# Half-array turns of the attention probabilities, beside the scores, and a new order of slots

## What is computed

```python
x = x + tanh(g_xattn[1]) * _L1_xattn_ref(_layernorm(x), ctx, ctx, Wq, Wk, Wv, Wo, bo)
#   16 heads of 64: attn = softmax(q @ k.T * 64**-0.5); out = concat(attn @ v) @ Wo + bo
x = x + tanh(g_ffn[1]) * _L1_ffn_ref(_layernorm(x), centroids, biases, Ws_up, Ws_down, W_up, W_down)
#   shared = silu(x @ Ws_up) @ Ws_down; top 8 of 64 experts by x @ centroids.T; weighted sum
```

## Time and profile before

| | us |
|---|---|
| median of 3 runs | 2946.25 (2937.28 to 2954.1) |
| profiled execution, span from first to last instruction | 2561.4 |
| outside the span, by the median | 384.85 |
| PE busy | 2366.4 (92% of the span) |
| DVE busy | 1692.1 (66%) |
| ACT busy | 1525.4 (60%) |
| POOL busy | 729.2 (28%) |

### The profile page before, as it was taken

The page is one execution under the profiler, slowest core; times in us unless marked ns, Lnnn a source line. Parts: engine busy times, 40 slices in busy tenths (PEclk is TensorE's granted clock), DMA queues, the critical chain, the costliest instruction groups (busy, mean ns, idle before and its releaser), DMA issues. The chain is left out here.

```text
span 2561.4 us, 63498 instructions
## 1 busy us (share of the span) xinstructions
PE 2366.4 (92%) x20058; PEld 1795.7 (70%) x20059; DVE 1692.1 (66%) x5327; ACT 1525.4 (60%) x4611; POOL 729.2 (28%) x863
## 2 busy tenths in 40 slices
PE   7999999999998999999999999999999869999950
PEld 5777777777776566666666666666666658888840
DVE  4776776777674567767667767766776645555559
ACT  3777777777773656656666666665665425545530
POOL 2000000000000023322322332332332347777740
PEclk8999999999999999999999999999999989999975
DMA  5111111111113211111111111111110366666659
GB/s 155 44 36 48 46 36 48 45 42 42 45 35 95 72 30 47 42 35 41 42 40 37 42 44 32 47 42 30 47 42 28 110 211 187 186 186 188 188 186 380
DMA packets 145288, 210.06 MB, mean 82 GB/s; under 512 B 23976, under 2 KB 108506, under 8 KB 145026
## 3 DMA queue, kind: packets, MB, share of 16 engines
q1 hardware_dynamic: 114322, 139.92, 18.7%
q0 software_dynamic: 26544, 60.21, 7.0%
q10 hardware_dynamic: 4160, 6.55, 0.7%
HBM read 118.21 MB, written 96.75 MB: 84 GB/s over the span
## 5 line engine op out<-in xcount | busy, mean ns | idle before, releaser
L1454 ACT ACTIVATE wup<-bank,nmax 112x375 f32<-112x375 f32 x512 | 297.3, 585 | 127.2 <-DVE nmax L1558 126.0
L766 ACT ACTIVATE prob<-bank,nmax 112x375 f32<-112x375 f32 x512 | 293.6, 586 | 55.7 <-DVE nmax L850 51.6
L850 DVE TENSOR_REDUCE nmax<-bank 112x1 f32<-112x375 f32 x512 | 255.4, 541 | 90.2 <-PE bank L588 90.2
L2045 POOL DMA_INDIRECT expert_results<-res,dest x288 | 280.2, 973 | 118.5 <-ACT res L2163 67.0
L1558 DVE TENSOR_REDUCE nmax<-bank 112x1 f32<-112x375 f32 x512 | 255.4, 541 | 36.0 <-PE bank L1250 36.0
L1895 POOL DMA_INDIRECT expert_rows<-rows,ids x248 | 237.2, 957 | 78.6 <-issue 69.0
L2163 ACT ACTIVATE res<-bank,xr 128x256 f32<-128x256 f32 x288 | 136.4, 474 | 190.7 <-PE bank L2077 189.6
L1868 POOL TENSOR_TENSOR stats<-stats,neg_half 112x1 f32<-112x1 f32 x64 | 35.7, 557 | 654.6 <-DVE stats L1589 652.2
L1313 PE MATMUL bank<-wup,wk 128*128 128x375 f32 x512 | 219.8, 512 | 2.1 <-DMA wup<-context_turned 0.9
L1019 POOL TENSOR_TENSOR stats<-stats,neg_half 112x1 f32<-112x1 f32 x64 | 35.1, 549 | 633.7 <-DVE stats L880 629.7
L1460 ACT COPY pT<-bank 128x336 f32<-128x336 f32 x512 | 201.1, 449 | 19.7 <-PE bank L1257 19.1
(11 more groups left out here) (255 smaller groups left out, 5001.6 us busy)
## 6 DMA issues: line engine op xcount, KB each, us to landing
xr<-expert_rows SPq DMA_DIRECT2D x288, 129.0 KB
wup<-expert_results SPq DMA_DIRECT2D x14, 1024.0 KB, 18.8
wdn<-expert_results SPq DMA_DIRECT2D x14, 1024.0 KB, 20.2
wdn<-in_L_ffn_W_down_dram SPq DMA_DIRECT2D x8, 1024.0 KB, 12.2
expert_rows<-nowhere SPq DMA_DIRECT2D x56, 129.0 KB, 3.1
x_and_h_in<-stage SPq DMA_DIRECT2D x32, 224.0 KB, 2.6
xt<-x_and_h_in SPq DMA_DIRECT2D x32, 224.0 KB, 2.8
context_turned<-ctxT SPq DMA_DIRECT2D x32, 187.5 KB, 2.3
```

The costliest lines, as they stand in the source:

```text
L766: nc.scalar.activation(prob[:, n % RING, :NK], s_bank[r][:NQ, :NK], ACT.Exp, bias=nmax[:, r:r + 1], accum_out=rsum[:, par, h:h + 1]).then_ ...
L850: nc.vector.tensor_reduce(nmax[:, r:r + 1], s_bank[r][:NQ, :NK], AX, ALU.max, negate=True).then_inc(maxed, 1)
L1454: nc.scalar.activation(prob[:, n % RING, :NK], s_bank[r][:NQ, :NK], ACT.Exp, bias=nmax[:, r:r + 1], accum_out=rsum[:, par, n:n + 1]).then_ ...
L2045: nc.gpsimd.indirect_dma_start(results_d, bass.IndirectOffsetOnAxis(ap=dest[:, n % DEST:n % DEST + 1], axis=0), res[:, n % RES, :], None, ...
```

## The change

Turning goes by two heads at once, and in two halves: rows 0 to 63 and 64 to 111 of the probabilities are turned separately, each in its half of the array's rows, into a bank of its own (bank 4 takes six blocks of 64 columns, bank 5 six of 48). ACT copies each bank in one instruction for both heads. A quarter begins with the turns of two heads, then come the next scores, then the turns of the other two, and all slots follow. `ORDER_C` is laid anew (no job changes its lane; no slot n of a quarter is used). ACT takes the router's exponential out of the router's slot to the end of the third quarter; DVE takes the four maxima of a quarter in one piece ahead of the slots, and `shared_silu` goes from slot 9 to 11.

```diff
 ORDER_C = [
-    (1, "post", "va3", "dve"), (1, "own", "v10", "act"), (1, "own", "v11", "dve"),
+    (1, "post", "va3", "dve"), (1, "own", "v10", "act"), (1, "post", "wo", "dve"), (2, "own", "v12", "act"),
...
-                def turn(i, n):
-                    wait_kept(pe, i, n - 1)
-                    pe.wait_ge(exped, H * i + n + 1)
-                    for c in range(KC):
-                        mm = pe.transpose(pt_bank[n % 2][:, c * NQ:(c + 1) * NQ],
-                                          prob[:, n % RING, c * P:(c + 1) * P], ident[:NQ, :NQ])
+                def turn_pair(i, n):
+
+                    wait_kept(pe, i, n)
+                    pe.wait_ge(exped, H * i + n + 2)
+                    for a in range(2):
+                        for c in range(KC):
+                            at = a * KC + c
+                            for half, rows_of in enumerate((slice(0, HALF_Q), slice(HALF_Q, NQ))):
+                                width = rows_of.stop - rows_of.start
+                                mm = pe.transpose(pt_bank[half][:, at * width:(at + 1) * width],
+                                                  prob[rows_of, (n + a) % RING, c * P:(c + 1) * P], ident[rows_of, rows_of])
                     mm.then_inc(turned, 1)
...
                         uses.run(hooks, i, n, par, first, last)
+                        turn_pair(i, n)
                         next_scores(i, par, g, last)
+                        turn_pair(i, n + 2)
                         uses.run(hooks, i, n + 1, par, first, last)
-                        turn(i, n)
-                        turn(i, n + 1)
                         uses.run(hooks, i, n + 2, par, first, last)
-                        turn(i, n + 2)
-                        turn(i, n + 3)
                         uses.run(hooks, i, n + 3, par, first, last)
...
+                    to = pT[:, n % PT_RING:n % PT_RING + 2, :].rearrange("p a (c q) -> p (a c) q", c=KC)
+                    for half, (start, stop) in enumerate(((0, HALF_Q), (HALF_Q, NQ))):
+                        width = stop - start
+                        nc.scalar.copy(to[:, :, start:stop],
+                                       pt_bank[half][:, :2 * KC * width].rearrange("p (a q) -> p a q", q=width)).then_inc(kept, 1)
...
+                        uses.run(hooks, i, n, par, first, last)
+                        keep_pair(i, n)
+                        keep_pair(i, n + 2)
+                        next_exponentials(i, par, n, last)
+                        uses.run(hooks, i, n + 1, par, first, last)
+                        next_exponentials(i, par, n + 1, last)
                         tanhs(i, n, last)
...
+                        next_exponentials(i, par, n + 2, last)
                         uses.run(hooks, i, n + 2, par, first, last)
-                        next_exponentials(i, par, n + 2, last)
                         next_exponentials(i, par, n + 3, last)
-                        tanhs(i, n + 3, last)
+                        if n == 8 and not first:
+                            sigmoid_exp(i - 1)
                         uses.run(hooks, i, n + 3, par, first, last)
...
-                parts_y = [(2, moments_y), (4, norm_y), (9, choose), (11, sigmoids), (12, weigh), (9, shared_silu),
+                parts_y = [(2, moments_y), (4, norm_y), (9, choose), (11, sigmoids), (12, weigh), (11, shared_silu),
...
-                        next_maximum(i, par, n, last)
-                        next_maximum(i, par, n + 1, last)
-                        next_maximum(i, par, n + 2, last)
+                        for m in range(4):
+                            next_maximum(i, par, n + m, last)
```

More of the change, by code:

```diff
@@ L33 @@
 ORDER_C = [
-    (1, "post", "va3", "dve"), (1, "own", "v10", "act"), (1, "own", "v11", "dve"),
[L35 to L42, removed]
+    (1, "post", "va3", "dve"), (1, "own", "v10", "act"), (1, "post", "wo", "dve"), (2, "own", "v12", "act"),
+    (2, "own", "v11", "dve"), (3, "own", "r0", "act"),
+    (5, "own", "va0", "dve"), (5, "pre", "k4", "act"), (5, "post", "lnT", "dve"), (6, "pre", "k1", "act"),
+    (6, "pre", "xT", "dve"), (6, "pre", "k0", "act"), (7, "pre", "k2", "dve"), (7, "own", "r1", "act"),
+    (7, "pre", "k3", "dve"), (7, "pre", "k7", "act"),
+    (9, "own", "va1", "dve"), (9, "pre", "q0", "act"), (9, "post", "router", "dve"), (10, "post", "shared_up", "act"),
+    (10, "pre", "v00", "dve"), (11, "pre", "k5", "act"), (11, "own", "r2", "act"),
+    (13, "own", "va2", "dve"), (13, "own", "r3", "act"), (13, "post", "rank", "dve"), (13, "pre", "q1", "act"),
+    (14, "post", "shared_down", "dve"), (14, "pre", "v01", "act"), (15, "pre", "k6", "dve"), (15, "pre", "v02", "act"),
 ]
@@ L1072, in layer1_phase @@
     PT_RING = 8
-    DVE_KEEPS = ()
+    HALF_Q = P // 2
     N_ROUTER = 11
@@ L1094, in layer1_phase, with pairs @@
         assert place(one) < place(other)
[L1096 to L1100, removed]
+    def pairs(i, n):
+        return (H * i + n) // 2
     with ExitStack() as es:
@@ L1158, in layer1_phase @@
         scored, maxed, exped = sem("scored"), sem("maxed"), sem("exped")
-        turned, kept_dve, kept_act = sem("turned"), sem("kept_dve"), sem("kept_act")
+        turned, kept = sem("turned"), sem("kept")
         inverted, expanded = sem("inverted"), sem("expanded")
@@ L1170, in wait_kept @@
         def wait_kept(eng, i, n):
-            by_dve, by_act = kept(i, n)
-            wait(eng, kept_dve, by_dve)
-            wait(eng, kept_act, by_act)
+            wait(eng, kept, 2 * pairs(i, n))
         def freed(eng, j, name):
@@ L1226, in _ @@
                 experts_up(1)
-                sp.wait_ge(turned, H * NB)
+                sp.wait_ge(turned, pairs(NB, 0))
                 experts_up(2)
@@ L1452, in exponentials, with keep_pair @@
                         wait(act, inverted, NT * (i - 1))
-                    wait(act, turned, H * i + n + 1 - RING)
+                    if isinstance(i, int) and H * i + n >= RING:
+                        act.wait_ge(turned, pairs(i, n - RING) + 1)
                     nc.scalar.activation(prob[:, n % RING, :NK], s_bank[r][:NQ, :NK], ACT.Exp, bias=nmax[:, r:r + 1],
                                          accum_out=rsum[:, par, n:n + 1]).then_inc(exped, 1)
-                def keep_turned(i, n):
-                    act.wait_ge(turned, H * i + n + 1)
+                def keep_pair(i, n):
+                    act.wait_ge(turned, pairs(i, n) + 1)
                     room_in_pT(act, i, n)
-                    nc.scalar.copy(pT[:, n % PT_RING, :], pt_bank[n % 2][:, :KC * NQ]).then_inc(kept_act, 1)
+                    to = pT[:, n % PT_RING:n % PT_RING + 2, :].rearrange("p a (c q) -> p (a c) q", c=KC)
[3 more added lines that the diff above has]
+                                       pt_bank[half][:, :2 * KC * width].rearrange("p (a q) -> p a q", q=width)).then_inc(kept, 1)
                 def q(g):
@@ L1511, in _ @@
                 hooks |= {f"v{half}{c}": v(half, c) for half in range(2) for c in range(KC) if uses.lane[f"v{half}{c}"] == "act"} | {f"r{g}": inverse(g) for g in range(NT)}
-                hooks |= {"router": lambda p, par, n: sigmoid_exp(p), "shared_up": shared_exps}
+                hooks |= {"shared_up": shared_exps}
                 tanh_h(0)
@@ L1769, in inverses @@
                 def inverses(i, par, n):
-                    for v, at in enumerate((0, 7, 8, 12)):
+                    for v, at in enumerate((0, 4, 8, 12)):
                         if n == at:
@@ L1785, in body @@
                         parts(i, n + 1, par, first, last)
-                        next_maximum(i, par, n + 3, last)
                         inverses(i, par, n + 2)
```

17 lines of the change are left out of this document (1 added, 16 removed).

## The result

The changed kernel takes 2922.58 us (median of 6 runs, 2920.02 to 2929.93), the kernel before 2941.02 (6 runs, 2936.49 to 2954.1): ratio 0.9935 [0.9917, 0.9954], 0.65% faster. Forecast were 3062 us and a range of 2938 to 3115: wrong in sign, and outside the range.

The account below looks back on a forecast made before the run. PE was taken to bound layer 1 at 37.84 us a sequence; its work falls to 35.2, waits rise to 6.4, giving 41.6, 3.75 more, over 31 sequences +116 us: 2946 + 116 = 3062 us, range 2938 to 3115.

Parts of the forecast that it names:

- what lies outside it up to the median of the runs, 385 us, I leave as it is: Time between the profiled span of 2561 us and the timed median: 385 us, taken as untouched by the change.
- `lnT`: Second quarter: PE waits about 1.5 us before `lnT` because DVE comes late, in place of `k1`'s .64.
- `k0`: Second quarter: PE waits .64 us before `k0` for its bank, with only `xT` between `k1` and it.
- `k3`: Second quarter: PE waits .51 us before `k3` for the bank of `k2`, with only `r1` between.
- `r2`: Third quarter: PE waits .83 us before `r2` for the bank of `k5`, with nothing between.
- `rank`: Fourth quarter: PE waits 1.2 to 1.4 us before `rank` because DVE comes late, in place of .35.
- half turns: PE's turns: .36 us for two heads in place of .57, saving 1.7 us a sequence.
- changes of shape: PE drains between whole-array and half-array work: .20 us each, 12 a sequence in place of 15, .6 less.
- Rival 1: PE's turns: halves do not pay, .64 or .57 us for two heads; 3115 to 3130 us, chance 10%.
- Rival 2: Layer 1: banks turn round inside other work, waits stay .35 us a sequence, 71 us saved: 2875 us, chance 15%.
- Rival 3: Layer 1: a wash, DVE not late and ACT copies sooner, waits 2.2 to 3.1: 2932 to 2960 us, chance 11%.
- Rival 4: Layer 1: PE's granted clock falls to .50 after idling, at most 31 us more; left out, no separate chance.

Follow-up runs that it names:

- before_again: The kernel before, unchanged, run and profiled again: 2926.23 us, ratio 1.0007 to the kernel before.
- after_again: The changed kernel, unchanged, run and profiled again: 2904.07 us, ratio 0.9935 to the kernel before.
- after_paced: The changed kernel with each scatter of a sequence's rows waiting for the landing of the one ahead: 2830.22 us, ratio 0.9673 to the kernel before.
- order_alone_paced: The changed kernel with whole turns in place of half turns, and one scatter of a sequence's rows in flight at a time: 2850.66 us, ratio 0.9756.
- halves_alone: The kernel before, in its old order of slots, with turns done and copied in halves: 2930.64 us, ratio 1.0025 to the kernel before.
- before_paced: The kernel before with each scatter of a sequence's rows waiting for the landing of the one ahead: 2718.10 us, ratio 0.9297.
- before_paced4: The kernel before with the fifth of a sequence's eight scatters waiting for the landing of the first four: 2705.74 us, ratio 0.9251.
- order_alone: The changed kernel's new order with whole turns, one ACT copy a head, scatters unpaced: 2852.46 us, ratio 0.9756 to the kernel before.

## Why the prediction was wrong

The step that failed is "what lies outside it up to the median of the runs, 385 us, I leave as it is". Of the 364.8 us between the profile of before (2561.4) and before_again (2926.2), 235.8 lie ahead of the 31st `wo` (2249.56 against 2013.79), 127.1 behind it, and 1.9 outside the span. The 235.8 are, but for 3.1 ahead of the first `wo`, hold-ups inside the stage that the change rearranges, and it takes most of those away. The 127.1 lie in the main behind that stage: 121 of them between the first and the last scatter of results (505.2 us against 384.2), and the change leaves those (505.1 in after_again). In the stage 7.8 us a sequence become 2.9, while its own work and waits cost 3.68 more (41.78 against 38.10). 7.8 - 2.9 - 3.7 = 1.2 us a sequence gained; over 29 sequences 35 us, less 3.6 in the first one: 31. Of these 22 show in the medians (2926 against 2904) and 25.6 in the spans, where the first `wo` comes 3.0 later and what follows the 31st is 2.8 longer. So the sign was lost on a term that the forecast carried along without a look inside it.

The working for an execution without a hold-up stands, term by term (first sequence of the changed kernel, start to next start less the job's own time):

| | forecast | measured |
|---|---|---|
| sequence | 41.6 | 41.16 |
| `lnT` | 1.5 | 900.67 - 898.21 - .63 = 1.83 |
| `k0` | .64 | 902.29 - 901.57 - .19 = .53 |
| `k3` | .51 | 904.47 - 903.75 - .19 = .53 |
| `r2` | .83 | 914.86 - 913.50 - .63 = .73 |
| `rank` | 1.2 to 1.4 | 919.99 - 918.70 - .19 = 1.10 |
| two heads turned in halves | .36 | .42 |

With r1 .20, `shared_up` .40, `v01` .37 and `v02` .21 the waits are 5.9 (forecast 6.4), and 41.16 - 5.9 = 35.3 for PE's work (forecast 35.2). That the work agrees so well is partly luck, since two of its terms are off: the half turns by 8 x .06 = .5 too short, the changes of shape by up to 12 x .10 = 1.2 too long.

- Half turns: right in kind, over-sized. Rival 1 falls: a pair takes .42 / 6 = .07 us. Eight times .57 - .42 is 1.2 us a sequence, not 1.7. In the new order they are worth 42.27 - 41.15 = 1.1 us in the first sequence and .7 in the paced ones, since PE then waits longer for DVE (`lnT`'s wait is 65.6 us in after_paced, 49.6 in order_alone_paced). Beside back-to-back scatters they cost: 2904 us with them, 2852 without. The Trainium skill, "TensorE: Matmul & The Clock Gate", section "LDWEIGHTS (loading the stationary operand)", gave .64 for two heads, an estimate; the trace has .42. Since a pair takes .07 and whole turns stand .096 apart, the rows of two halves do load side by side.
- Changes of shape: over-sized. halves_alone has some sixteen more of them in a sequence and saves 8 x (.57 - .42) = 1.2 in turns; its first sequence is .43 longer (37.99 against 37.56), so a change costs about .10 there, an estimate, not .20.
- Rival 2 (waits do not come): wrong; they came. Rival 3's 2932 to 2960 us lie nearest to the result, by another mechanism: DVE is late, as forecast.
- Rival 4: right as a mechanism, but the idle that lowers the clock is the hold-up's (.91 over before's sequences, .96 over the changed kernel's), not a wait of the new order: without a hold-up the first sequence runs at 1.00.

What stays open: why the profiled execution of before, alone of all, met no hold-up; why in the new order the late update falls on ACT's copies with half turns and hardly with whole ones; and what the late updates wait behind. The Trainium skill, "NOTIFIC — the notification-queue block", section "7.1 Overflow: three behaviours, one of which stalls the engine", says that the block which writes the records of a trace presses back, rather than lose a record inside itself, and that a count of such stalls above nothing would mean that an engine was slowed by it. The traces bear on this without settling it. The landings of eight scatters make 128 updates. The profile of before has 121 to 128 of them on record in a sequence, before_again 30 to 49, before_paced all 128, before_paced4 47 to 64, and order_alone, which loses .4 us, 25 to 48. So beside back-to-back scatters records are missing in every one of these executions but the first, with a hold-up or without. Whether the hold-up belongs to the recording, no run here can show: every run of the experiments has a span and a granted clock beside its time, so none is known to have gone unrecorded, and what pacing gains is shown for such executions alone.

## What to carry to other kernels

Where the span of a profile and the timed median of the same program differ by far more than usual (here 385 us, against 2 between span and time of the other profiled runs), suspect that the profile is not of an execution like the timed ones: look for the missing time inside the stages first, and give the change a term for it. A sequence that lacks one ingredient (here the first, without scatters) hints in one row at what that ingredient costs the others. Where DMAs go out back to back, try one wait for a landing in the middle of the burst: here it was worth more than any order of the compute (7.5%, in runs that may all have been recorded).

## What the runs showed of the hardware that I had not expected

- Beside eight scatters issued 1.26 us apart, semaphore updates passed slowly until the scatters had landed: some seven of SyncE's fifty took about 700 ns in place of 17; one of PE's reached DVE 6.03 us late (1487.35, for a product that ended at 1481.32). The profile of before has the same bursts without this. With four in a burst and a wait for their landing the loss is .9 us a sequence in the old order (38.46 against 37.56 in the first), and 2.1 with half turns.
- More updates in that stretch cost time: 50 more cost 3.1 to 3.35 us a sequence beside back-to-back scatters, and nothing (42.46 against 42.48) beside paced ones.
- Twelve transposes of 64 and 48 rows in the two halves of the array follow one another at .035 us (.42 / 12), loads of 128 columns included.
